# A fused decoder layer on one core: activation tables loaded by themselves, two groups of normalisations on GpSimd, and a new order of every engine's calls

## The reference, cut to what matters

```python
x = _layernorm(x + self_attention(x))      # sigmoid(qn kn^T / 16 - log 1024) v, q and k normalised, no mask
x = _layernorm(x + cross_attention(ctx, x))  # 16 heads of 16, softmax over 77 keys
x = _layernorm(x + channel_mix(x))         # sigmoid(xr W_r) * (relu(xk W_k)^2 W_v), xr and xk mix x with the row before
```

## Time and profile before

| | us |
|---|---|
| median of 3 runs | 535.18 (534.74 to 535.26) |
| span of the profiled execution | 531.8 |
| what lies around the span (median less span) | 3.4 |

### The profile page before, as it was taken

How to read it: one execution, slowest core, us unless ns; L and a number is a source line. 1 busy time by engine, 2 the same in 40 slices (tenths; PEclk the granted TensorE clock), 3 DMA queues, 4 the chain that set the end, 5 groups by cost and what they waited for, 6 DMA issues and landing times.

```text
span 531.8 us, 12709 instructions
## 1 busy us (share of the span) xinstructions
PE 515.0 (97%) x4530; PEld 468.3 (88%) x4530; DVE 443.7 (83%) x995; ACT 450.4 (85%) x1130; POOL 381.9 (72%) x554
## 2 busy tenths in 40 slices
PE   9999999999999999999999999999999898999994
PEld 6888999898989898989898989999898787899994
DVE  4787868878888879797979797778878888999996
ACT  3765579998989898989898989899999899898965
POOL 1774747676867676767667675767778889897996
PEclk9999999999999999999999999999999999999998
DMA  6410120110010110101010100020511000011122
GB/s 193 128 49 21 38 60 6 42 39 2 14 50 27 35 38 24 42 19 52 12 39 3 39 2 22 21 74 28 166 35 41 2 2 1 22 41 41 41 80 100
DMA packets 23269, 22.50 MB, mean 42 GB/s; under 512 B 1724, under 2 KB 23204, under 8 KB 23205
## 3 DMA queue, kind: packets, MB, share of 16 engines
q1 hardware_dynamic: 22770, 21.35, 12.7%
q10 hardware_dynamic: 434, 0.34, 0.2%
HBM read 14.55 MB, written 6.82 MB: 40 GB/s over the span
## 4 chain that ended last, share of the span: by engine, by line
PE 70%; ACT 12%; DVE 9%; issue 4%; POOL 4%; POOLq 0%; DVEq 0%; ACTq 0%
PE st L298 16%; PE acc L298 14%; PE xb L298 10%; PE proj L298 10%; PE xb L2077 5%; PE xb L2096 5%; ACT p_sb L594 4%; PE xb L2064 4%; DVE xm L1485 3%; ACT L545 2%; PE proj L1973 2%; PE xb L1885 1%; POOL rs L1110 1%; PE st L1893 1%; DVE kkT_lo L1299 1%
## 5 line engine op out<-in xcount | busy, mean ns | idle before, releaser
L594 ACT ACTIVATE p_sb<-xb,neg_mx 128x77 f32<-128x77 f32 x512 | 120.0, 366 | 5.2 <-DVE neg_mx L1412 4.9
L1047 POOL TENSOR_TENSOR fold<-p_sb 128x640 f32<-128x640 f32 x32 | 50.2, 1568 | 75.4 <-ACT p_sb L594 75.1
L1052 POOL TENSOR_TENSOR p_sb<-p_sb,rc 128x1280 f32<-128x1280 f32 x32 | 75.3, 2353 | 23.8 <-DVE rc L1425 23.7
L298 PE MATMUL acc<-vv_hi,aT_hi 128*128 128x256 f32 x256 | 76.6, 299 | 0.0
L545 ACT ACT_TABLE_LOAD x58 | 74.4, 1283 | 1.0
L298 PE MATMUL st<-qkT_hi 128*128 128x256 f32 x256 | 74.8, 292 | 0.0
L298 PE MATMUL st<-qkT_lo,qkT_hi 128*128 128x256 f32 x256 | 72.4, 283 | 0.0
L298 PE MATMUL st<-qkT_hi,qkT_lo 128*128 128x256 f32 x256 | 72.4, 283 | 0.0
L298 PE MATMUL acc<-vv_lo,aT_hi 128*128 128x256 f32 x256 | 72.2, 282 | 0.0
L298 PE MATMUL acc<-vv_hi,aT_lo 128*128 128x256 f32 x256 | 72.2, 282 | 0.0
L1412 DVE TENSOR_REDUCE neg_mx<-xb 128x4 f32<-128x308 f32 x128 | 53.7, 467 | 17.1 <-PE xb L2064 16.7
(11 more groups left out here) (262 smaller groups left out, 1707.9 us busy)
## 6 DMA issues: line engine op xcount, KB each, us to landing
xs<-in_x SPq DMA_DIRECT2D x16, 256.0 KB, 3.0
xraw<-in_xT SPq DMA_DIRECT2D x15, 256.0 KB, 2.9
out_y<-y SPq DMA_DIRECT2D x15, 256.0 KB, 2.1
x_kept<-xs SPq DMA_DIRECT2D x10, 256.0 KB, 2.2
x2s_a<-x_kept SPq DMA_DIRECT2D x2, 512.0 KB, 5.0
x2s_b<-x_kept SPq DMA_DIRECT2D x2, 512.0 KB, 7.1
x2s_c<-x_kept SPq DMA_DIRECT2D x1, 512.0 KB, 3.7
cT<-in_cT SPq DMA_DIRECT2D x1, 308.0 KB, 3.3
```

Of the source, the lines that this page charges most:

```text
L298: mm = pe.matmul(out, s_, m_, start=first and k == 0 and q == 0, stop=last and k == n - 1 and q == 2, skip_group_check=not check)
L594: ex = act.activation(weights(t)[:, h // KH * (H // 2) + KH * n + h % KH, 0:SC], logits[n][:, h * SC:(h + 1) * SC], ACT.Exp, bias=neg_mx[: ...
L1047: pool.tensor_tensor(fold[:].rearrange("p (h k) -> p h k", k=FO), p[:, :, 0:FO], p[:, :, FO:2 * FO], ALU.add).then_inc(fo_pool.sem, 1)
L1052: pool.tensor_tensor(weights(t), weights(t), rc[:, t % 2].rearrange("p (h o) -> p h o", o=1) .to_broadcast([P, H, SP]), ALU.mult).then_inc ...
```

## The change

It has four parts. `table_for` writes the load of the table alone, without the activation of one column. `N1` goes from 11 to 3 and `N2` from 7 to 0: `norm1` of pairs 3 to 10 and `norm2` of pairs 0 to 6 move from ScalarE to GpSimd. The first activation of the program, a copy of one column behind a wait for constants, is replaced by the load of the sigmoid's table. And all four lists of calls are written in another order, rounds included.

```diff
-N1 = 11
+N1 = 3
-N2 = 7
+N2 = 0
...
                     if loaded[0] != func:
                         loaded[0] = func
-                        w.wait_ge(*consts_pool.at(0))
-                        n = 8 * (next(spares) % NSPARE)
-                        act.activation(spare[:, n:n + 1], nlogs[:], func)
+                        act.preload_act_table(func)
...
-                w.wait_ge(*consts_pool.at(0))
-                act.activation(spare[:, 8 * NSPARE - 1:], nlogs[:], ACT.Identity)
+                table_for(ACT.Sigmoid)
                 act.dma_start(columns[:], io["columns"]).then_inc(load_id.sem, 16)
                 first_x_hi(0)
+                qk_biases()
+                wqk_hi(1)
                 first_x_hi(1)
-                wqk_hi(1)
...
 TensorE, the beginning:
                 warm_up()
+                on_all_rows(0)
+                on_all_rows(1)
                 first_qk()
-                on_all_rows(0)
                 qk(2)
                 qk(3)
-                on_all_rows(1)
...
 TensorE, a round (before: every call through at(), the same calls):
                 def round_(r):
+                    weights_t(2 * r - 13, 2)
+                    qk(2 * r)
+                    mixed(r - 7)
+                    v(r)
+                    cross_scores(2 * r - 11)
+                    attend(4 * r - 16)
+                    scores(4 * r - 13)
+                    weights_t(2 * r - 12, 0)
+                    scores(4 * r - 12)
+                    tqk(2 * r)
+                    dense(r - 7)
+                    x1(r - 5)
+                    qk(2 * r + 1)
+                    weights_t(2 * r - 12, 1)
+                    query(r - 5)
+                    weights_t(2 * r - 12, 2)
+                    attend(4 * r - 15)
+                    cross_scores(2 * r - 10)
...
 TensorE, the end:
+                attend(62)
                 cross_scores(28)
-                x2(1)
-                attend(62)
+                receptance(0)
                 weights_t(27, 0)
+                x2(2)
                 weights_t(27, 1)
                 weights_t(27, 2)
+                mixed(13)
                 attend(63)
-                mixed(13)
                 cross_scores(29)
+                receptance(1)
                 mix_keys(0)
-                receptance(0)
...
                 query(15)
-                weights_t(28, 2)
+                mix_values(0)
                 cross_scores(30)
-                mix_values(0)
                 mix_keys(1)
```

1362 lines of the change are left out of this document (846 added, 516 removed).

## The result

The changed kernel takes **572.32 us** (median of 4, 570.34 to 574.06), beside 535.22 us for the kernel before on the same chip (534.74 to 535.88). The ratio is **1.0692, 95% interval 1.0667 to 1.0716**: 37.1 us slower. The prediction said 531.7 us, with 528.0 to 535.8 as its range. It is wrong by more than its range and wrong in its sign.

A forecast was written before the change was run, and what follows sets the result against it. TensorE was taken to bound the rounds, and VectorE together with it from 454 us on. Terms 0.6 + 0.9 + 0.4 + 1.6 = 3.5 us took the span from 531.8 to 528.3, the median from 535.2 to 531.7 us; range 528.0 to 535.8.

The forecast's parts named there:

- What bounds the kernel: Whole span: TensorE's matmuls set the pace in the rounds, other engines have room; from 454 us VectorE bounds too.
- I take the round as unchanged, 25.9 us: Rounds in the new order: same matmuls, tightest distance `x1` to `query` still covered by 0.2 us, so no change.
- Rival C: Rounds: GpSimd's `norm2` meets VectorE's `x1_lo`, 0.36 us in each of 7 rounds, 2.5 us, 534.2; chance 0.07.
- The normalisations: nothing: Pairs 0 to 10: moving normalisations from ScalarE to GpSimd gains nothing by itself, since TensorE bounds that stretch.
- The tables: 0.9 us: Table switches on ScalarE: 8 on the chain each save 0.11 us without the activation; bounds nothing and 1.6 us.
- The beginning: 0.6 us: First projections: row sums placed ahead remove a wait of 0.5 to 0.6 us; lower bound nothing.
- The end: 0.4 + 1.6 us: After the rounds: last logits 0.4 us earlier, and 1.6 us less for VectorE where it bounds, `mixes(3)` moving ahead.
- near 446: Sign at the end: the sums of tile 31 would start near 446 instead of 448.07.
- Rival D: Rounds: ScalarE 1.3 us late at `x1_hi`, TensorE stands still before `query` in 7 rounds, 7.6 us, 539.3; chance 0.10.
- the 27 named as a sign of this rival: Rounds: starts of `mixed` 27 us apart, with a wait on `x1T_lo`, would show ScalarE late at `x1_hi`.

The follow-up runs named there:

- norms_only: Kernel before, own order, with norm1 of pairs 3 to 10 and norm2 of pairs 0 to 6 moved to GpSimd: 535.41 us, ratio 1.0013.
- fills_after: Changed kernel with GpSimd's long SBUF-reading instructions replaced by constant fills of the same places and nearly the same length: 534.94 us, ratio 0.9992.
- the five executions of the late kind: Profiled executions of five variants of the changed kernel: row sums 0.86 us apart, first projection began at 9.0 us.

## Why the prediction was wrong, step by step

**What bounds the kernel** was read rightly for before and did not hold after: "VectorE 22.18, GpSimd 17.93: all of them have room". Busy time is not room where two engines exclude each other. What counted was where GpSimd's gaps stood, and the prediction took them for idle time.

**"I take the round as unchanged, 25.9 us"** is the step that failed most. It compared what stands between a call and the call that needs it, with the durations of the old trace. That comparison was right: without the exclusion the rounds of the new order take 25.9 us; with it they took 26.9. But it compared each engine's list with its own old list, and took durations as fixed. It never laid VectorE's list beside GpSimd's. The rows for it were at hand: `qk_deviation(2r+9)` is followed at once by `residual2`, `residual1` and `xt_lo`, and by nothing that waits, and VectorE's next call needs exactly what `qk_deviation` makes. The same step, durations taken as fixed, stands under the terms for the beginning and the end, and cost more there: of the 35.9 us by which `mixed(15)` is later than with fills, 7.0 are in the rounds, 10.0 ahead of them and 18.9 behind.

**Rival C** named the mechanism and put it in the wrong place and size: `norm2` beside `x1_lo`, 0.36 us in 7 rounds, 2.5 us. By the rule of the Trainium skill that stood beside it (SBUF — State Buffer, section "SBUF: two separate sides") the meeting costs at `aT_lo` and not at `x1_lo`. With this the trace agrees: `x1T_lo` has a mean of 684 ns as before, `aT_lo` 1119 for 767. The failure was to price the rule for the two moved instructions only, and not for all of GpSimd's, which the new order had moved too. The norms in themselves met `qk_sb` 16 times in `norms_only` and lengthened it by 1.4 us in all.

**"The normalisations: nothing"**: right. `norms_only` is 0.7 us slower.

**"The tables: 0.9 us"**: right within its bounds; measured 0.5 us. ScalarE got back 6.1 us of busy time, where the prediction had 6.4.

**"The beginning: 0.6 us"**: wrong in sign. The wait that it removed was real, but the projections then ran at the lower clock level, and VectorE's first call, `bv_wide`, was overlooked. With the fills `mixed(0)` is 1.7 to 3.0 us late, in single executions.

**"The end: 0.4 + 1.6 us"**: cannot be seen in the changed kernel, where sums 31 started at 484.4 us and not near 446. Without the exclusion, from `mixed(0)` to sums 31 the new order takes 343.2 us against 345.0, 1.8 us less, where the prediction had 0.4 and up to 0.9 of the tables. From there to the end, where it had the 1.6 us less for VectorE, it takes 85.5 against 83.8, 1.7 us more. Together the two terms gave 0.1 us of their 2.0, by one execution of each. Why was not tried.

**Rival D** (ScalarE late at `x1_hi`) did not come: ScalarE waited for `x1`, 12.2 us in all, and TensorE waited for `x1T_lo` once, 0.5 us. That the rounds took 26.9 us, near the 27 named as a sign of this rival, is chance: the waits were for `qk_sb` and `aT_lo`.

**A second loss on top of the first** is the clock. After the stop of 2.77 us shown above the granted clock is at its lower level (windows of 2 us of after, PE, PEld, DVE, ACT, POOL, clock):

```profile
324.00:326.00 2.00, 0.53 (x3) 0.53 (x4) 2.00 (x3) 0.16 (x1) 2.00 (x2) 0.83 0.00 0
326.00:328.00 2.00, 2.00 (x11) 2.00 (x10) 2.00 (x8) 2.00 (x10) 0.55 (x1) 0.50 0.00 0
328.00:330.00 2.00, 2.00 (x16) 2.00 (x15) 2.00 (x5) 1.90 (x8) 0.00 (x0) 0.81 0.03 8
```

11 matmuls began where 19 had in 318 to 320. This happened at three stops (near 84, 326 and 463 us), and the windows of 10 us around them have a granted clock of 0.83, so each cost at most 0.17 of 10, 1.7 us. By the spacing of the products of 256 columns alone (40 times 0.213 us in place of 0.119) TensorE was slower by 3.8 us in all; the bounds are 4 and 5 us of TensorE's time, of which not all need have reached the end. It is a part of the 35.4: `fills_after`, without the stops, has no such windows between 20 and 520 us.

## What to carry to other kernels

When an order of calls is changed, lay the lists of VectorE and GpSimd side by side: for each VectorE instruction whose tensors are both in SBUF, ask what GpSimd does at that moment, and count up to the length of GpSimd's instruction for each meeting. A gap of GpSimd in a tuned kernel may be what keeps VectorE at its speed, so moving work into it is no gift, and a share of busy time says nothing about it: GpSimd's went from 72% to 74%. The test for it is cheap: put fills of the same length in place of GpSimd's reading instructions, and see whether the time falls.

## What the runs showed of the hardware

A constant fill on GpSimd does not hold up a VectorE subtraction of two SBUF tensors (686 ns against 684), but it does hold up a multiply-add or a copy of one SBUF tensor to another: eight multiply-adds of 542 ns have a mean of 696 beside four fills, and single copies take 0.82 us in place of 0.42. The form that looks lighter, one tensor read, is thus the more exposed one; it was still worth 2.1 us with the tables (0.5 of them the tables' own), and I put that down to its being shorter. And in the five executions of the late kind the granted clock reads 1.00 between 4 and 14 us while products of 512 columns are 0.43 us apart, so at a program's start the durations have to be read, not that column.
